# Inverse norms of seven units on ScalarE with a Newton step on VectorE, and the second layer's low parts on GpSimd

## The reference

```
q = heads(x @ W_q); k_t, v_t = heads(text @ W_k), heads(text @ W_v)
probs_t = softmax(q k_t^T / 4)
text_out = probs_t v_t
qsem = l2norm(probs_t @ text)              # one vector of 512 per query and head
sem = qsem @ l2norm(ip)^T                  # 4 image tokens
probs_ip = softmax(q k_ip^T / 4 + 0.5 * sem) * spatial_mask
out = (text_out + probs_ip v_ip) @ W_out + b_out + x
```

## Time and profile before

| | us |
|---|---|
| median of 3 runs | 797.25 (794.05 to 798.55) |
| the profiled execution, its own time | 792.34 |
| its span, first to last instruction | 790.5 |
| TensorE busy in the span | 733.6 |
| VectorE busy | 567.5 |
| ScalarE busy | 425.6 |
| GpSimd busy | 394.9 |

### The profile page before, as it was taken

The page is one execution under the profiler, slowest core; times in us unless marked ns, Lnnn a source line. Parts: engine busy times, 40 slices in busy tenths (PEclk is TensorE's granted clock), DMA queues, the critical chain, the costliest instruction groups (busy, mean ns, idle before and its releaser), DMA issues.

```text
span 790.5 us, 17597 instructions
## 1 busy us (share of the span) xinstructions
PE 733.6 (93%) x6452; PEld 570.5 (72%) x6452; DVE 567.5 (72%) x1579; ACT 425.6 (54%) x915; POOL 394.9 (50%) x297
## 2 busy tenths in 40 slices
PE   5879899999999989998999999999999999988796
PEld 5767677878787867777776777777877777646474
DVE  5357375857667575958779788698797887786765
ACT  5225556464637464655465555555755646445551
POOL 5512221020202040204388877778769769779873
PEclk9999999999999999999999999999999999999999
DMA  9967834765638472927264254343442612500010
GB/s 274 236 186 178 217 114 123 226 147 181 177 109 223 113 189 85 248 77 187 72 149 133 65 142 154 84 127 114 119 125 71 149 64 64 143 1 17 21 34 17
DMA packets 104356, 101.90 MB, mean 129 GB/s; under 512 B 10408, under 2 KB 103504, under 8 KB 104272
## 3 DMA queue, kind: packets, MB, share of 16 engines
q1 hardware_dynamic: 103632, 100.46, 46.5%
q10 hardware_dynamic: 640, 0.33, 0.2%
HBM read 61.67 MB, written 36.74 MB: 124 GB/s over the span
## 4 chain that ended last, share of the span: by engine, by line
PE 68%; DVE 13%; ACT 5%; issue 4%; DMA 3%; POOL 3%; ACTq 2%; SPq 2%; POOLq 0%; DVEq 0%
PE pB L395 20%; PE pB L542 13%; PE pB L626 5%; PE pB L522 4%; PE pB L492 4%; PE pPV L574 4%; PE pPV L564 3%; PE pPV L569 3%; PE pB L583 3%; ACTq L803 2%; PE pB L527 2%; PE pPV L560 2%; DVE m_sb L1130 2%; DVE Y L1146 2%; DVE cc L1030 1%
## 5 line engine op out<-in xcount | busy, mean ns | idle before, releaser
L1384 POOL TENSOR_TENSOR Y<-P,wkv 128x512 f32<-128x512 f32 x160 | 207.4, 1319 | 110.6 <-ACT P L905 110.5
L542 PE MATMUL pB<-wkv 128*128 128x512 f32 x560 | 147.7, 402 | 9.9 <-DVE ipS L1132 5.9
L542 PEld LDWEIGHTS pB<-wkv 128*128 128x128 f32 x560 | 100.5, 188 | 41.1 <-DVE ipS L1132 10.5
L1130 DVE TENSOR_REDUCE m_sb<-pB 128x2 f32<-128x504 f32 x160 | 106.8, 674 | 31.8 <-PE pB L492 31.5
L1360 POOL TENSOR_TENSOR klo<-xin,khi 128x256 fp32r<-128x256 f32 x18 | 13.2, 751 | 220.9 <-ACT khi L810 220.9
L1146 DVE TENSOR_TENSOR Y<-pB,Y 128x512 f32<-128x512 f32 x160 | 104.8, 682 | 25.5 <-PE pB L542 20.9
L895 ACT ACTIVATE wkv<-pB 128x512 fp32r<-128x512 f32 x160 | 86.5, 594 | 52.0 <-PE pB L522 32.5
L905 ACT ACTIVATE P<-pB 128x512 f32<-128x512 f32 x160 | 86.7, 599 | 50.5 <-PE pB L522 27.0
L905 ACT ACTIVATE P<-pB,ln 128x512 f32<-128x512 f32 x160 | 101.4, 694 | 0.0
L810 ACT ACTIVATE Vs<-pPV 128x512 f32<-128x512 f32 (+1 forms) x80 | 39.2, 490 | 105.7 <-PE pPV L574 63.0
L1128 DVE TENSOR_REDUCE m_sb<-pB 128x2 f32<-128x358 f32 x160 | 83.4, 521 | 0.0
(11 more groups left out here) (161 smaller groups left out, 1297.0 us busy)
## 6 DMA issues: line engine op xcount, KB each, us to landing
QP<-q0d SPq DMA_DIRECT2D x64, 192.0 KB, 4.3
KP<-k0d SPq DMA_DIRECT2D x64, 192.0 KB, 4.9
c_sb<-in_cT SPq DMA_DIRECT2D x16, 512.0 KB, 5.2
q0d<-qhi SPq DMA_DIRECT2D x32, 256.0 KB, 2.8
k0d<-khi SPq DMA_DIRECT2D x32, 256.0 KB, 2.4
q0d<-qlo SPq DMA_DIRECT2D x16, 256.0 KB, 3.0
k0d<-klo SPq DMA_DIRECT2D x16, 256.0 KB, 2.5
VB<-vipd SPq DMA_DIRECT2D x6, 640.0 KB, 4.5
```

The lines of the kernel that those rows point to most:

```text
L542: made = mm(bank[:, :], G[i][:, col:col + 128], ph[:, src, :, :].rearrange("p a s -> p (a s)"), start=(n == 0), stop=(n == len(jobs) - 1))
L1130: nc.vector.tensor_reduce(m_sb[:, :, h], v[:, :, 0:TXT1], AX, ALU.max)
L1384: tt(y, w, r.bitcast(F32), SUB).then_inc(po_y, 1)
```

## The change

Three things are changed.

1. The inverse norms of units 8 to 14. GpSimd's power is gone for these seven units (unit 15 keeps it). VectorE forms n2 once for all 20 heads, in slot 0 of the next unit. In slot 1, right behind the exponentials of pair q+1, ScalarE takes the logarithm of n2 and an exponential of it ("inv"). VectorE refines the result by three small operations at the start of "soft" ("refine"), where before it waited for GpSimd.
2. The exponential ex moves from the end of slot 1 to slot 2, right behind the exponentials of pair q+1 there ("ex").
3. The low parts of context and input for units 10 to 15 go from VectorE to GpSimd: two (of x) in slot 8 and four (of the context) in slot 9 of units 7 to 12. VectorE keeps the third part of x.

```diff
 def norm_parts(u):
-    return {g: (4 * g, 4 * g + 4) for g in range(NG)} if u == U - 1 else {3: (0, 16), 4: (16, H)}
+    return {g: (4 * g, 4 * g + 4) for g in range(NG)} if u == U - 1 else {NG - 1: (0, H)}
...
     weights = [("weights", q + 1, halves)] if scores else []
+    if u > B and j == 1:
+        weights += [("inv", u - 1)]
+    if u > B and j == 2:
+        weights += [("ex", u - 1)]
...
+            def inverse_norms(u):
+                k = u - B
+                ac.wait_ge(dv_n2, k + 1)
+                ac.wait_ge(dv_st, k)
+                act(rn[:, :, :], n2[:, :, :], ACT.Ln, scale=2.0 ** 16).then_inc(ac_ln, 1)
+                ac.wait_ge(ac_ln, k + 1)
+                act(rn[:, :, :], rn[:, :, :], ACT.Exp, scale=-0.5, bias=ln256).then_inc(ac_rn, 1)
...
-                        elif what == "soft":
+                        elif what == "inv":
+                            inverse_norms(*a)
+                        elif what == "ex":
                             image_weights(*a)
...
         def low_c(u):
-            return 0 < u < B + 2
+            return u > 0
...
             def split_x(u):
-                ks = (2,) if 0 < u < B + 2 else range(KC)
+                ks = (2,) if u else range(KC)
...
+            def refine(u):
+                dv.wait_ge(ac_rn, u - B + 1)
+                then(tt(e2[:, :, :], n2[:, :, :], rn[:, :, :], MUL))
+                settled()
+                then(stt(e2[:, :, :], e2[:, :, :], -0.5, rn[:, :, :], MUL, MUL))
+                settled()
+                then(stt(rn[:, :, :], e2[:, :, :], 1.5, rn[:, :, :], ADD, MUL))
+                settled()
...
-                dv.wait_ge(po_rn, norms_no(u, NG - 1))
+                if u == U - 1:
+                    dv.wait_ge(po_rn, NG)
+                else:
+                    refine(u)
...
-                        elif what == "back" and a[0] >= B and a[1] in norm_parts(a[0]):
+                        elif what == "back" and a[0] == U - 1:
                             norms(*a)
...
-                        elif what == "x" and 0 < a[0] < B + 2:
+                        elif what == "x" and a[0] > 0:
                             split_x(*a)
```

More of the change, by code:

```diff
@@ L61, in norm_parts @@
 def norm_parts(u):
-    return {g: (4 * g, 4 * g + 4) for g in range(NG)} if u == U - 1 else {3: (0, 16), 4: (16, H)}
+    return {g: (4 * g, 4 * g + 4) for g in range(NG)} if u == U - 1 else {NG - 1: (0, H)}
 def norms_no(u, g):
-    return 2 * (u - B) + list(norm_parts(u)).index(g) + 1
+    return u - B + list(norm_parts(u)).index(g) + 1
 def folded(u):
@@ L221, in build @@
         y21 = sb("y21", [128, 32])
-        ln2 = sb("ln2", [128, 1])
+        logs = sb("logs", [128, 2])
+        ln2, ln256 = logs[:, 0:1], logs[:, 1:2]
         flat = lambda a: a[:, :, :, :].rearrange("p a b c -> p (a b c)")
@@ L295, in build @@
             sem(f"pe_{n}") for n in ("nt", "sr", "ot", "wt", "op", "mb", "ip"))
-        ac_x, ac_c, ac_exp, ac_ph, ac_bg, ac_vs, ac_sr, ac_ot, ac_wt, ac_ex, ac_mb, ac_w, ac_set, ac_ip = (
-            sem(f"ac_{n}") for n in ("x", "c", "exp", "ph", "bg", "vs", "sr", "ot", "wt", "ex", "mb", "w", "set", "ip"))
+        ac_x, ac_c, ac_exp, ac_ph, ac_bg, ac_vs, ac_sr, ac_ot, ac_wt, ac_ex, ac_mb, ac_w, ac_set, ac_ip, ac_ln, ac_rn = (
+            sem(f"ac_{n}") for n in ("x", "c", "exp", "ph", "bg", "vs", "sr", "ot", "wt", "ex", "mb", "w", "set", "ip", "ln", "rn"))
         dv_q, dv_mx, dv_bg, dv_fix, dv_y, dv_nb, dv_o, dv_n2, dv_st, dv_sr, dv_ot, dv_op, dv_bd, dv_add, dv_f, dv_wt, dv_set, dv_ip, dv_vg, dv_ic = (
@@ L897, in weights @@
             def weights(q, halves):
-                twice = {"bias": ln2[:, 0:1]} if q >= B * NP else {}
+                twice = {"bias": ln2} if q >= B * NP else {}
                 for n in range(2):
@@ L1277, in vector_program @@
             nc.vector.memset(ones, 1.0)
-            nc.vector.memset(ln2[:, :], float(np.log(2.0)))
+            nc.vector.memset(ln2, float(np.log(2.0)))
+            nc.vector.memset(ln256, float(np.log(256.0)))
             then(nc.vector.memset(y21[:, :], 0.0))
```

## The result

The changed kernel takes 808.09 us in the median of 4 runs (804.78 to 812.63), against 797.02 for the kernel before (4 runs): ratio 1.0178, 95% interval 1.0138 to 1.0217. It is slower by 11.1 us, in place of the 15.5 predicted. The profiled execution took 804.78 us, with a span of 802.6 us, 12.1 more than before, and a mean granted clock of 0.980 against 0.991. TensorE has the same 6452 matmuls as before and is busy 4.6 us longer with them (733.6 us before).

A forecast was written before the change was run, and what follows sets the result against it. TensorE was taken as the bound nearly everywhere in layer 1. Five units at +4.6 us (+23), low parts -5.0, unit 14 +0.2 and unit 15 -2.7 gave +15.5: 812.5 us, range 799 to 827.

The forecast's parts named there:

- The block: idle time: Slot 1, units 9 to 13: two table loads and two activations on ScalarE delay qhi, Y and TensorE's L574 by 3.2 us.
- dear loads: Rival: each table load holds ScalarE for about twice 1.283 us, a block costs 5.6, total 829 us; chance 0.14.
- free loads: Rival: loads run beside ScalarE's activations, qhi is delayed only 0.5 us a block, total about 792 us; chance 0.08.
- Newton and the clock: Units 9 to 13: VectorE's three refining operations add 0.72 us, clock falls in rather more than half the units 0.7 each.
- Low parts, -5.0: Low parts moved to GpSimd remove six of TensorE's waits for VectorE at unit starts, -5.0 us in all.
- The rival that gave the relief of VectorE no worth: Rival: moving the low parts gains nothing and the clock falls in each unit, +24.6, total 822 us; chance 0.10.
- No wait of TensorE for the low parts is seen.: GpSimd's 4.6 us of low parts a unit stay covered; without cover, some tenths in a unit.
- Unit 14, +0.2: VectorE waits 0.8 us for rn and adds 0.72; some 1.3 comes back without GpSimd's power: +0.2 us.
- unit 15, -2.7: End of run: earlier rn lets L583 start about 741.5 instead of 744.6 and w's wait end sooner: -2.7 us.
- The sum: Whole run: 23.0 - 5.0 + 0.2 - 2.7 = +15.5 us, said as 812.5 us.
- The stall half made good: Rival: rested engines take away TensorE's other waits in the unit, a block costs no less than 2.7, 800 to 803; chance 0.12.

The follow-up runs named there:

- e3: Changed kernel without the Newton step's three operations, inverse norms left unrefined: 807.54 us, ratio 1.0166 to the kernel before.
- e5: Changed kernel with twelve unread matmuls ahead of TensorE's wait for Y in slot 2 of units 9 to 13: 807.23 us, ratio 1.0151 to the kernel before.
- e12: e9 with the low parts of units 10 to 15 back on VectorE: 796.12 us, ratio 1.0003 to the kernel before.
- e1: Kernel before with only the low parts of units 10 to 15 moved to GpSimd, powers kept: 804.27 us, ratio 1.0119 to the kernel before.
- e2: Changed kernel with the low parts back on VectorE, so the norms and moved ex alone: 814.02 us, ratio 1.0235 to the kernel before.
- e9: Changed kernel with one table set for both functions loaded once at the start, the 14 loads gone: 792.48 us, ratio 0.9970 to the kernel before.
- e13: e11 without the Newton step, norms not refined: 786.11 us, ratio 0.9880 to the kernel before.
- e11: e9 with the two small activations moved behind the qhi copies of slot 1, "soft" left in place: 791.51 us, ratio 0.9966 to the kernel before.

## Why the prediction was right, step by step

**The block: idle time.** Predicted 3.2 us between P and the next instruction, carried through to L574. TensorE's wait grew from 0.26 to 3.46: 3.20. The load's row gave its full cost, as the earlier trace rows had it. The Trainium skill, page "ScalarE: Activation LUTs", section "What ACT_TABLE_LOAD costs", adds a drain of some 1380 ns to each switch; the trace shows the load's 1283 ns of that page and no drain, since the activation starts 0.01 us behind it. The rival of dear loads falls with this row, and so does that of free loads.

**Newton and the clock.** Predicted 0.72 + 0.7 = 1.4 a unit; measured 4.45 - 3.20 = 1.25, where 4.45 is the growth of unit 11, 3.63, plus the 0.82 given back. The sum holds, but its parts don't add as I had them. The clock falls in all five units, not in rather more than half, and the step lies wholly beneath it: without the step the unit is 0.06 shorter (e3), and with the clock kept up it is 0.8 shorter and shows 0.50 of the step (e5). The two are one cost of which the larger counts: the 1.28 us by which TensorE's busy time grows in unit 11 are the whole of it. The price of a fall was also bounded too low, at 1.7: in unit 9 the clock stays low for twice as long, and busy time grows by 2.2 (52.93 to 55.13). The step's own price at full clock is 0.5, not 0.72, because some of it fits into VectorE's slack.

**Low parts, -5.0.** The size came out right by luck, and the reason was wrong. All six waits are gone: 1.25 and 0.46 at the starts of units 8 and 9, and 0.82 at those of units 10 to 13. But in the last four, 3.3 us together, the giver is the removal of GpSimd's power, which the prediction booked at nothing except as room for the low parts. e12 keeps the low parts on VectorE and those waits are gone all the same; e1 moves them with the power in place and loses 1 us in a unit. Only the first two, 1.7 us together, are the low parts' own: with these back on VectorE they return (1.24 and 0.54 in e12, 0.99 and 0.54 in e2). The totals show the coupling as well: the low parts alone cost 1.19% (e1), the norms alone 2.35% (e2), the two together 1.78%. The step failed where it read "VectorE is the cause of the wait" from the wait's releaser, and did not ask why four operations with 410 ns each take 2.51 us in the earlier trace rows. The prediction knew of slow operations beside GpSimd, since it used them in unit 14, and did not look for them here. The rival that gave the relief of VectorE no worth had this right for units 10 to 13, and the fall of the clock in each unit too; its time was missed because the power's removal gave the four waits back.

**"No wait of TensorE for the low parts is seen."** True in the changed kernel. The price if the cover were gone was given as some tenths a unit; e1 shows 1.0 to 1.3 in units 10 to 12, through VectorE and not through Y, and 2.96 once for GpSimd's klo, which no term had.

**Unit 14, +0.2, and unit 15, -2.7.** VectorE waited 0.66 for rn in unit 14, where 0.8 was predicted; TensorE's waits over 0.2 us there sum to 6.90, against 6.73 before. In unit 15 the three waits shrank by 2.73, in other shares than told: the one for Vs, which was to go, is still 0.87, the one for w grew from 1.31 to 1.63, and the one for Y is gone. From unit 13 on the run is +0.75, against 4.6 - 0.82 + 0.2 - 2.7 = +1.28 by the prediction.

**The sum.** By units the prediction says -1.2, +4.1, three times +3.78 and +1.28, together +15.5; measured -1.57, +3.89, +3.68, +3.63, +3.62 and +0.75, together 14.0. The terms were a little too large, 1.5 us in all; the rest of the difference to the 12.1 of the spans, 1.9, lies ahead of unit 8, where hardly anything was changed and TensorE's busy time differs by 2.09 for the same matmuls. That is the granted clock of that execution, and no term of the prediction. Kernels that are alike in this stretch differ more: unit 8 starts at 354.44 in e12, 358.38 in e9 and 362.25 in e13, with TensorE busy 327.23, 329.88 and 336.93 us before it.

**The stall half made good** is refuted: in units 10 to 13 TensorE lost no other wait but the one at their start. In unit 9 it lost two more, of 0.43 and 0.29, and the longer stretch of low clock took as much back, so that 3.89 for the 4.1 predicted there is in part luck.

## What to carry to other kernels

Before moving a function to ScalarE, count the table loads that the program gets between its activations, and load one set for all of them: here that is the whole difference between 1.0178 and 0.9970. A wait's releaser names who came last, not who made it late: compare the releaser's instructions with their own duration elsewhere, and look for the engine beside them. And when a stall lets the clock fall, small work right behind it can be free, as the Newton step was here, and show up again once the stall is mended; price such terms together.

## What the runs showed of the hardware

**GpSimd and VectorE hold each other up, for a whole instruction.** e11's unit 9, GpSimd and then VectorE:

```profile
420.26 1.56 POOL L1399 TENSOR_TENSOR wo<-c_sb,wo 128x640 fp32r<-128x640 f32 x1 [0.34 <-ACT wo L813]
...
420.17 0.20 DVE L1199 SCALAR_TENSOR_TENSOR e<-e,rn 128x40 f32<-128x40 f32 x1
420.41 1.47 DVE L1201 SCALAR_TENSOR_TENSOR rn<-e,rn 128x40 f32<-128x40 f32 x1
421.91 0.92 DVE L1211 TENSOR_TENSOR t<-ST,rn 128x160 f32<-128x160 f32 x1
```

VectorE's operation of 0.20 us takes 1.47 and ends at 421.88, GpSimd's at 421.82. Only unit 9 has this piece of GpSimd's work there, which is why the Newton step, a run of short operations with two operands in SBUF, the on-chip memory, costs 3.5 us in it and 0.5 elsewhere: TensorE then waits 3.43 for a bank (1.36 in e13), and the quad behind it is slow by the clock:

```profile
425.84 3.29 PE L545 MATMUL pB<-wkv 128*128 128x512 f32 x7 [3.43 <-DVE ipS L1147]
```

The Trainium skill, page "SBUF — State Buffer", section "SBUF: two separate sides", has the rule: of a GpSimd operation and a VectorE operation with two SBUF inputs, the one that starts first holds the shared ports for its whole length. The ends above agree with it, and it goes both ways: beside VectorE's operations GpSimd's product at 519.47 took 2.12 us (in the section on e2), where the mean is 1.32. In e11's unit 9 one copy with a single operand in SBUF (wvi from cc, 128x16) was held too, at 1.23 us in place of 0.17. VectorE's qlo and its products into Y, which have one operand in PSUM, where the banks are, keep their 0.69 and 1.28 us beside GpSimd in all runs.

**One set of tables serves both functions.** In e9, P's pair of exponentials takes 1.27 us as before. The same skill, page "ScalarE: Activation LUTs", section "Table sets: the hidden batching unit", says that one set has both; the runs agree, and show that this kernel had to ask for it.

**The clock.** A wait of some 3.45 us for Y brought the granted clock down to 0.50, which is 1.2 GHz, in each of the five units, for about 3.4 us in units 10 to 13 and 6.8 in unit 9; the waits of 0.74 and 0.50 of e9 left it up in units 10 to 13. In unit 9 a wait of 1.97 (e9) and one of 3.43 (e11) were followed by a fall, and one of 1.36 (e13) was not.
